# Two short contractions of a decoder-layer kernel read with all 128 rows, the unused weights zero

## The reference

```python
# state-space block: INNER 256, STATE 16, RANK 64
xpj = conv @ xproj_w                       # 64 + 16 + 16 columns
ts, Bm, Cm = xpj[..., :64], xpj[..., 64:80], xpj[..., 80:]
delta = softplus(ts @ dt_w + dt_b)         # dt_w is [64, 256]
state = exp(A * d_t) * state + d_t * B_t * h_t       # 64 steps in time
y = state . C_t + D * h_t
# feed-forward: 8 routed experts of 176 hidden features, top 2, and a shared one
eo = (silu(x @ wg[e]) * (x @ wu[e])) @ wd[e]
y = sum_e cw[e] * eo[e] + (silu(x @ wg_s) * (x @ wu_s)) @ wd_s
```

## Time and profile before

| | |
|---|---|
| three timed runs | 1900.26, 1901.47, 1901.95 us (median 1901.47) |
| span of the profiled execution, first to last instruction | 1896.3 us |
| mean granted TensorE clock in it | 0.952 of full speed |
| busy: TensorE matmul, TensorE weight load | 1679.0 us (89%), 960.4 us (51%) |
| busy: VectorE, ScalarE, GpSimd | 1504.8 us (79%), 1421.6 us (75%), 1548.3 us (82%) |
| DMA, mean of 16 engines | about 25% |

### The profile page before, as it was taken

How to read it: one execution, slowest core, us unless ns; L and a number is a source line. 1 busy time by engine, 2 the same in 40 slices (tenths; PEclk the granted TensorE clock), 3 DMA queues, 4 the chain that set the end, 5 groups by cost and what they waited for, 6 DMA issues and landing times. The chain is left out here.

```text
span 1896.3 us, 25668 instructions
## 1 busy us (share of the span) xinstructions
PE 1679.0 (89%) x7046; PEld 960.4 (51%) x7046; DVE 1504.8 (79%) x1890; ACT 1421.6 (75%) x4402; POOL 1548.3 (82%) x1284
## 2 busy tenths in 40 slices
PE   4678999999899999989999998999999899998976
PEld 1234454656545465654646565464655545465544
DVE  4888878888897888988788888879888897878332
ACT  5479687786978778797887869788787978767362
POOL 0678888989898888988888898888889898898734
PEclk7679999999999999999999999999999999999988
DMA  2312312222221212322121233212223321231102
GB/s 97 90 39 79 95 49 85 64 68 101 79 95 51 84 62 68 101 79 94 48 89 62 68 101 79 94 49 88 62 68 101 79 95 49 77 96 49 62 3 65
DMA packets 125918, 140.43 MB, mean 74 GB/s; under 512 B 44048, under 2 KB 69456, under 8 KB 125776
## 3 DMA queue, kind: packets, MB, share of 16 engines
q1 hardware_dynamic: 125776, 138.79, 24.4%
HBM read 133.77 MB, written 4.98 MB: 73 GB/s over the span
## 5 line engine op out<-in xcount | busy, mean ns | idle before, releaser
L1171 POOL TENSOR_TENSOR prod<-state,c_rep 128x1024 f32<-128x1024 f32 x256 | 610.0, 2385 | 36.7 <-PE p_y L629 18.7
L1034 DVE TENSOR_TENSOR_SCAN state<-decay,p_drive 128x1024 f32<-128x1024 f32 x256 | 584.6, 2284 | 26.1 <-ACT decay L771 12.8
L771 ACT ACTIVATE decay<-delta,a_neg 128x504 f32<-128x504 f32 x512 | 360.1, 721 | 51.8 <-DVE state L1034 50.5
L629 PE MATMUL p_y<-prod,ident 128*128 128x512 f32 x768 | 397.3, 610 | 0.0
L1024 DVE TENSOR_TENSOR p_drive<-u,p_drive 128x1024 f32<-128x1024 f32 x256 | 312.7, 1221 | 66.7 <-PE p_drive L617 66.4
L903 ACT ACTIVATE ex<-p_ring,nmax 128x64 f32<-128x64 f32 x1024 | 307.4, 368 | 2.9 <-DVE nmax L1086 2.3
L903 ACT ACTIVATION_READ_ACCUMULATOR ex<-p_ring,nmax 128x1 f32 x1024 | 253.7, 262 | 0.0
L729 PE MATMUL p_ring<-x2T,wg 128*128 128x512 f32 x416 | 234.6, 665 | 3.6 <-ACT us L955 3.6
L729 PE MATMUL p_ring<-x2T,wu 128*128 128x512 f32 x384 | 200.8, 621 | 31.8 <-DVE km L1145 19.4
L1224 POOL TENSOR_TENSOR ex<-ex,rden 128x512 f32<-128x512 f32 x128 | 144.9, 1132 | 81.0 <-DVE rden L1090 80.7
L943 ACT ACTIVATE gt<-p_ring 128x512 f32<-128x512 f32 (+1 forms) x208 | 123.8, 596 | 116.3 <-PE p_ring L729 113.1
(11 more groups left out here) (141 smaller groups left out, 3110.5 us busy)
## 6 DMA issues: line engine op xcount, KB each, us to landing
c_rep<-c_rows SPq DMA_DIRECT2D x256, 256.0 KB, 3.6
cwr<-cw_rows SPq DMA_DIRECT2D x64, 256.0 KB, 3.4
ctxT<-in_ctx_t SPq DMA_DIRECT2D x32, 256.0 KB, 5.5
cwr<-cw_rows SPq DMA_DIRECT2D x32, 224.0 KB, 2.9
cwr<-cw_rows SPq DMA_DIRECT2D x32, 192.0 KB, 2.8
cwr<-cw_rows SPq DMA_DIRECT2D x32, 160.0 KB, 3.0
xf<-in_x SPq DMA_DIRECT2D x16, 256.0 KB, 4.4
xb<-in_x SPq DMA_DIRECT2D x16, 256.0 KB, 4.7
```

Of the source, the lines that this page charges most:

```text
L629: pe.matmul(p_y[1 - first][:], ident[:], prod[:, slot_of(c, n), 1 - first, :], start=False, stop=n == STATE - 1, skip_group_check=True).th ...
L771: act.activation(decay[:, n % 2, j, :].rearrange("p (b t) -> p b t", t=SEQ)[:, :, 1:], delta[:, c.parity, j, :].rearrange("p (b t) -> p b ...
L1034: dve.tensor_tensor_scan(state[:, slot_of(c, n), :, :].rearrange("p j t -> p (j t)"), decay[:, n % 2, :, :].rearrange("p j t -> p (j t)"), ...
L1171: pool.tensor_tensor(mine, state[:, slot_of(c, n), :, :], c_rep[:, n % C_SLOTS, :].unsqueeze(1).to_broadcast([128, HALVES, T]), ALU.mult). ...
```

## The change

`wdt` gets 128 rows, the lower 64 of them zeros from the host, and the dt matmuls read all 128 rows of `xp_sb`. The last tile of the down projection is read with all 128 rows; its weights' rows 48 to 127 were zeros before (`pad`), and VectorE now clears `acts[12]` once at the start, so that rows 48 to 127 hold zeros. Nobody else writes these rows.

```diff
--- before.py
+++ after.py
@@ -362,7 +362,7 @@
         rowb = sb("rowb", [128, 2, D])
         win = sb("win", [128, 4, 128])
         wxp = sb("wxp", [128, HALVES, 128])
-        wdt = sb("wdt", [RANK, INNER])
+        wdt = sb("wdt", [128, INNER])
         wout = sb("wout", [128, HALVES, D])
         wattn = sb("wattn", [128, 4, 128])
         wrt = sb("wrt", [128, EXPERTS])
@@ -662,7 +662,7 @@
                                        start=j == 0, stop=j == HALVES - 1)
                 elif name == "dt":
                     pe.wait_ge(xp_ready.sem, xp_ready.at(c.m))
-                    mm = pe.matmul(p[:], wdt[:, i * 128:(i + 1) * 128], xp_sb[0:RANK, :], start=True, stop=True)
+                    mm = pe.matmul(p[:], wdt[:, i * 128:(i + 1) * 128], xp_sb[:], start=True, stop=True)
                 elif name == "mout":
                     pe.wait_ge(xb_ready.sem, xb_ready.at(c.m))
                     pe.wait_ge(yg_ready.sem, yg_ready.at(c.m, 1))
@@ -744,10 +744,9 @@
                                 pe.wait_ge(gu_ready.sem, gu_ready.at(c.m, ON_POOL.index(SPLIT)))
                             elif i == 0 and g == 0 and j >= ROUTED:
                                 emptied(pe, "up_u", j, c.m)
-                            rows = slice(0, REST if j == SPLIT else 128)
                             mm = pe.matmul(p[:, g * D:(g + 1) * D],
-                                           acts[j][rows, (2 * i + g) * 128:(2 * i + g + 1) * 128],
-                                           wd[rows, j, :], start=False, stop=j == FFN_TILES - 1)
+                                           acts[j][:, (2 * i + g) * 128:(2 * i + g + 1) * 128],
+                                           wd[:, j, :], start=False, stop=j == FFN_TILES - 1)
                 mm.then_inc(ring_full[r].sem, 1)
 
             turns("pe", step)
@@ -996,6 +995,7 @@
             dve.tensor_scalar(a_neg[:].rearrange("p a n -> p (a n)"), a_neg[:].rearrange("p a n -> p (a n)"),
                               -1.0, None, ALU.mult).then_inc(consts_v.sem, 1)
             dve.memset(decay[:], 0.0)
+            dve.memset(acts[SPLIT], 0.0)
             dve.memset(vm[:], 0.0)
             dve.memset(r_sel[:, :, EXPERTS:], TOP_EPS)
             dve.memset(r_cw[:], 0.0).then_inc(consts_v.sem, 1)
@@ -1320,7 +1320,7 @@
         "ctx_t": np.asarray(ctx_1024).reshape(BATCH * SEQ, D).T,
         "vec": vec, "rows": rows,
         "w_in": np.asarray(L0_attn_in_w).reshape(128, 4, 128),
-        "w_xproj": xproj, "w_dt": np.asarray(L0_attn_dt_w),
+        "w_xproj": xproj, "w_dt": np.concatenate([np.asarray(L0_attn_dt_w), np.zeros((128 - RANK, INNER), np.float32)]),
         "w_out": np.asarray(L0_attn_out_w).reshape(HALVES, 128, D).transpose(1, 0, 2),
         "w_attn": attn, "w_router": np.asarray(L0_ffn_w_router).T,
         "w_gate": gate_tiles, "w_up": up_tiles[:, :SPLIT, :],
```

## The result

| | before | after |
|---|---|---|
| median of the timed runs, us | 1900.87 (1899.33 to 1901.95) | **1854.76** (1852.91 to 1860.94) |
| span of the profiled execution, us | 1896.3 | 1858.9 (device time 1860.94) |
| mean granted clock in it | 0.952 | 0.965 |
| q0 of chunk 2 to q0 of chunk 13, us | 1216.10 | 1191.15 |

The ratio is 0.9764, 95% interval 0.9747 to 0.9781: 2.4% faster. Forecast were 1875 and a range of 1858 to 1892, so the direction was right, but the gain is 46 us instead of 26, and 3 us past the range. The execution that was profiled is the longest of the four; the other three have spans of 1850.8 to 1853.8 us.

What follows compares the result with a forecast made beforehand. TensorE's time behind a fall of its clock was taken to set the turn. Eleven turns gain 22 us, outside some 4.5: 26.5 off the 1896.3 span gives 1869.8, plus 5.2 makes 1875 us; range 1858 to 1892.

Steps and rivals of the forecast that it cites:

- The bound and the clock: Behind a drop of TensorE's clock to half near dt, TensorE sets the turn; full dt rows would keep the clock up.
- The first rival: Only the short tiles' edges go and the clock still falls at dt: 1888 us, chance 0.20.
- the change does nothing: Rival: slow steps beside short tiles have another cause, or every microsecond turns into another wait: 1901 us, chance 0.06.
- The slower rival: With down earlier, the clock falls in the score stage too, while falls at dt stay: 1909 us, chance 0.04.
- all goes through: Rival: VectorE and GpSimd move along with TensorE, so every gain passes: 1843 to 1858 us, chance 0.07.
- turns under 107.5: Sign against the prediction: turns shorter than 107.5 us would say VectorE and GpSimd were no bound.
- Down edges: Slow steps around the 48-row down tile, 1.52 us a chunk; 0.5 passes, as GpSimd's km then holds score0.
- dt edges: Slow steps around dt's 64-row matmuls: 0.36 us a turn, bounds 0.19 and 0.38, passing to the turn.
- The falls: Drops of TensorE's clock to half around dt: two of three go, one of three stays, no long turn left.
- second piece: The second 3.41 us at half clock in a long turn: its removal is worth 1.67 us, in four turns.
- Outside: Gain outside the eleven turns, from the last two chunks' down and neighbouring turns, less the memset: some 4.5 us.
- What lies around the span: The 5.2 us by which the median of the runs is above the profiled span, added to the forecast span.

Runs made afterwards that it cites:

- e1: The kernel before with only dt read with 128 rows, the last down tile still read with 48: 1879.18 us, ratio 0.9876.
- e3: The changed kernel with both dt and the last down tile read with 72 rows instead of 128: 1864.20 us, ratio 0.9801.
- e5: The changed kernel as it is, timed again: 1855.80 us, ratio to the kernel before 0.9782.
- e6: The changed kernel with one added full product, result overwritten, in TensorE's wait ahead of the second x2 transpose: 1847.13 us, ratio to the kernel before 0.9738.
- e2: The kernel before with only the last down tile read with 128 rows, dt still read with 64: 1872.96 us, ratio 0.9845.
- e4: The kernel before with one added full product, result overwritten, in TensorE's wait ahead of the second x2 transpose: 1880.98 us, ratio 0.9887.
- e10: The changed kernel as it is, timed a third time: 1856.60 us, ratio to the kernel before 0.9765.
- e9: The changed kernel with dt alone read with 72 rows, the last down tile kept at 128: 1862.66 us, ratio to the kernel before 0.9795.

## Why the prediction was right and wrong

**The bound and the clock: right.** Behind a fall TensorE's time is the turn's time, the falls depended on dt's rows, and full rows removed falls. The first rival (edges only, falls stay) is excluded by e1, which changes dt alone and has 2 falls of 11 where there were 11. That the change does nothing is excluded by both lengths of turns. The slower rival needed falls in the score stage: the three profiled executions of the changed kernel have none there in the eleven turns, and the one that was met (e3, 6.8 us behind q0) left its turn at 107.8. In them a fall at another place did come once, at down0 in the turn behind the eleven in e5, and that turn took 109.86 us against 106.99 in e6.

The result lies in the span given to *all goes through* (1843 to 1858, chance 0.07), and its mechanism, "VectorE and GpSimd turn out to move along with TensorE", is what the runs show for the down edges. It isn't so for dt's edges, and 3 to 6 of eleven falls stayed. The prediction's own sign that VectorE and GpSimd were no bound, turns under 107.5, came as well (107.24 in this execution, 107.03 in e5). It came from the down edges; that the two do hold TensorE up is shown by its 1.22 us of waiting for r_cw.

**Down edges: the size right, what passes wrong.** "So of 1.52 I take 0.5 through". It is 1.3, the largest error: 0.8 x 11 = 9 us. The step that failed is GpSimd's end of km (810.21), taken as fixed when down gets shorter, "without having waited for down1". What the changed kernel does there (timeline, ScalarE, GpSimd, TensorE):

```profile
899.80 1.04 POOL L1215 TENSOR_TENSOR km<-kT,masks 128x512 f32<-128x512 f32 x1
900.11 1.45 ACT L870 ACTIVATE qs<-p_ring,bqs,masks 128x512 f32<-128x512 f32 x2 [0.20 <-PE p_ring L682]
900.82 2.71 POOL L1218 TENSOR_SCALAR km<-kT,masks 128x512 f32<-128x512 f32 x4
901.45 1.94 ACT L891 ACTIVATE km<-kT,masks 128x512 f32<-128x512 f32 x3
903.79 1.10 PE L698 MATMUL p_ring<-km,qs 128*128 128x512 f32 x2 [0.90 <-POOL km L1218]
```

Measured from q0 (899.04), GpSimd ends km at + 4.49 (before + 3.94) and score0 starts at + 4.75 (before + 4.59). As forecast, score0 waits for GpSimd (L1218) and not for ScalarE. But GpSimd's part itself ends 1.0 us earlier, since q0 comes 1.52 earlier and it keeps all but 0.55 of that. So only 0.16 was lost between q0 and score0, and 1.36 of 1.52 is through there. GpSimd before, in the turn that follows the one of the earlier trace rows (q0 at 917.87), and after (timeline, GpSimd):

```profile
911.20 0.20 POOL L1189 TENSOR_TENSOR var<-mv,eps 128x2 f32<-128x2 f32 x1 [1.41 <-DVE mv L1012]
...
918.08 1.04 POOL L1215 TENSOR_TENSOR km<-kT,masks 128x512 f32<-128x512 f32 x1 [0.24 <-PE p_ring L748]
...
893.20 0.20 POOL L1189 TENSOR_TENSOR var<-mv,eps 128x2 f32<-128x2 f32 x1 [0.19 <-DVE mv L1012]
```

GpSimd did wait for down1, 0.24 us, in twelve of the thirteen turns from chunk 1's q0 to chunk 13's; the turn of the earlier trace rows is the one in which its earlier work ended late enough to hide it. In all thirteen it starts 0.21 or 0.22 behind q0, and the program says the same (its step `k` waits for `down` 1 of the chunk ahead). That is 0.24 of the 1.0. The other 0.74 comes from its work ahead of L1215, which is fed by down0 in its turn, through the sums that VectorE reads: GpSimd waited 1.41 us for them before and 0.19 after. After, it starts km right behind that work, at q0 + 0.76, and no longer waits for down1. A chain beside the one being shortened was treated as independent from one turn's rows, and it hangs on the same stage twice.

**dt edges: size and passage both wrong.** "I take 0.36 [...] and passes". It is 0.18 (2.87 to 2.69 us from route to the first up). That this meets the lower bound of 0.19 is luck: the bound was taken against full steps of 0.43, but four full ones in dt's place take 1.80 (950.49 to 952.29 above), not 1.72. Of the 0.18, 0.11 lie between dt and the first up, and 0.07 ahead of dt. And nothing passes. Without a fall, e2 with its short dt takes 107.4 twice and 108.1 once; the changed kernel takes 107.0 to 108.0 in 20 turns of its three executions, 107.5 on the mean. With one piece it is mostly 108.7 and 108.8. Where the down tile is short, a full dt even costs 0.2 (108.9 to 109.1 in e1, 108.72 in e4). Where dt is full, GpSimd starts 0.29 earlier (route + 8.54, in e2 + 8.83) and hits r_cw, so that cwT starts at + 10.0, in e2 at + 9.05. That was 4 us of forecast that does not exist, and in this execution some 2 more.

**The falls: the number too high, the worth too low.** Forecast were two of three gone and none long; found were 5 of 11, then 8 and 7 of 11 in e5 and e10, and none long in any. Right is that the second piece is worth 1.67. The first was put at 1.65 - 0.86 = 0.8, by the slack of VectorE; it is 1.2 (108.72 to 109.93 before; 107.6 to 108.79 after). At the third pair of ups, where the 0.7 was read, the kernel before does show about that: route + 12.1 with one piece, + 11.3 without (e4). The changed kernel shows nothing there: + 12.2 with a fall and without, because of r_cw, and TensorE's wait stayed at 0.61 where a longer one was the sign. The 1.2 comes behind it, from VectorE's delta and u (lines 1067, 1070) and GpSimd's sum of the scan (line 1176). The turn with the fall (route 840.81), then the one without (949.60):

```profile
854.71 2.36 POOL L1176 TENSOR_TENSOR prod<-prod 128x1024 f32<-128x1024 f32 x1
855.66 2.49 DVE L1067 TENSOR_TENSOR delta<-delta,sp_a 128x1024 f32<-128x1024 f32 x1
858.18 2.17 DVE L1070 TENSOR_TENSOR u<-delta,h 128x1024 f32<-128x1024 f32 x1
...
961.80 2.35 POOL L1176 TENSOR_TENSOR prod<-prod 128x1024 f32<-128x1024 f32 x1
964.48 1.21 DVE L1067 TENSOR_TENSOR delta<-delta,sp_a 128x1024 f32<-128x1024 f32 x1
965.73 1.23 DVE L1070 TENSOR_TENSOR u<-delta,h 128x1024 f32<-128x1024 f32 x1
```

VectorE begins delta at the same place, route + 14.9. With the fall GpSimd, fed 1.7 us later, is still at its sum, delta and u take 4.7 us instead of 2.4, and TensorE waits 1.50 for VectorE at the next pair (route + 20.2); without it the wait is 0.3 or none (+ 18.6 to + 19.1). So part of what a fall costs is paid in an overlap of two other engines, which lengthens their instructions and is no wait of theirs. (This is read from the rows; no run moves this overlap alone.)

**The eleven turns by the measured terms.** Down edges 11 x 1.3 = 14.3; dt -0.2 x 11 = -2.2 (this execution's turns without a fall are 107.6 on the mean, against 108.72 - 1.3); four second pieces 6.7; five first pieces x 1.2 = 6.0. Sum 24.8, measured 1216.10 - 1191.15 = **24.95**, forecast 22. Two errors of opposite sign hide each other here, 9 us too little for the down edges and 6 too much for dt, so that the nearness is luck; and in other executions of the changed kernel the eleven turns take 1185.97 and 1188.04.

**Outside: 4.5 forecast, 12.4 found.** q0 of chunk 2 is 7.80 us earlier (364.85 to 357.05). The two turns ahead of it, which the forecast gave some 2 us, are 4.2 and 4.0 shorter: before, they had stretches at 0.50 of 3.41 us at 193.24 and at 213.72 and one of 6.83 at 305.88, and after none of the three. The start costs 0.43, as forecast (0.48); the new memset and who waits behind it:

```profile
11.53 0.48 DVE L998 MEMSET acts_more<- 128x512 f32 x1
...
16.87 0.69 ACT L808 ACTIVATE hpad<-p_ring,vecs 128x512 f32<-128x512 f32 x1 [2.96 <-DVE r_cw L1001]
```

The end gave 4.6. The last 26 down instructions in the chain that ended last take 2.92 us instead of 3.11. From the first product of the last chunk's down in that chain to the end of the span it is 20.2 us (from 1838.68) instead of 22.4 (from 1873.91), so 2.1 lie there; what gives the other 2.5 was not followed.

```profile
1850.09 2.92 PE p_ring L747 x26
```

**What lies around the span: 5.2 us taken, 2.05 found.** In this execution device time and span differ by 2.05 us (1860.94 and 1858.9), and in all the others by 2.0 to 2.2. The 5.2 was the distance of one profiled execution's span from the median of others, and that execution was a quick one of its kind. Reading a difference between executions as a constant put 3 us on the forecast. The same confusion works the other way after: this profiled execution is 6 us above its median. The sum over the forecast's 1875: span 10.9 us too long, 3.1 around it, 6.2 between this execution and the median, 20.2 in all. Of the 10.9, 3 lie in the eleven turns and 7.9 outside.

**Open.** Which turn has a fall is read from where it stands (the table with e9), but not why a turn that stands there loses the clock. The windows above have 2.38 us busy ahead of a fall and 2.71 with none, but the kernel before had a fall behind 3.08 and none behind 1.93. And the end of a turn of 107.0.

## What to carry to other kernels

Before an edge is costed at what "the next waiter" leaves of it, follow that waiter's own feed back, in several turns and in the program's waits: if it comes from the stage that is being shortened, it moves too, here 1.3 of 1.52 us instead of 0.5. Pad contractions of 64 rows or fewer to full ones where the rows are there for nothing, and look in the windows whether TensorE's clock falls at them; then fill the wait ahead of them with work that is needed, or with a product that is thrown away. Time that an engine gains can start GpSimd early enough to stall a small VectorE instruction, and the gain is gone without any new wait in the program.

## What the runs showed of the hardware

- A float32 product of 48 or 64 rows among full ones costs time in the steps beside it: 0.38 us for each short tile of a down group (3.51 to 3.13), 0.18 for dt; nothing at 72 rows. In the down group four steps take 0.20 to 0.21 us from start to start instead of 0.11: into the short pair, between its two, out of it and the one behind. In dt the steps between the 64-row matmuls take 0.43 like full ones, except the first (0.53; 0.51 full), and the steps in and out are 0.07 and 0.09 longer.
- Rows matter to the granted clock: the stretch behind route in which a fall began was 0.88 to 3.23 us with dt at 64 rows, 0.88 to 2.66 at 72 and 0.75 to 1.82 at 128. In the eleven turns that made 11 falls at 64 rows (8 with the down part), 7 and 6 at 72, and 6, 3 and 4 at 128; with 64 and 72 rows some last 6.8 us, with 128 none does.
- One thrown-away product of 0.86 us ahead of the stretch took the changed kernel from 3 falls in the eleven turns to none, for 8.7 us over the whole.
- VectorE's products whose two operands both lie in SBUF wait out a GpSimd instruction that is already running: r_cw 0.19 or 1.16 us (128x32), r_prob 0.19 or mostly 1.1 to 1.4, delta 1.21 or mostly 1.9 to 2.5 (128x1024). The drive product, with one operand in PSUM and the same 128x1024, takes 1.22 in all its 256 records (1.204 to 1.230), nearly all of them beside GpSimd. The Trainium skill (SBUF — State Buffer, SBUF: two separate sides) has one port pair that both engines share as an exclusive lock, among others for a VectorE operation with two SBUF inputs, for the whole instruction of whoever starts first; the trace agrees with it in these numbers, and in the other order too: u at 965.73 took 1.23 us, and the GpSimd product (line 1249) that started 0.13 behind it 2.23 instead of 1.27.
